# First unit's stacks read in two goes, and the order of the first and last loads, in a four-layer transformer kernel

## The chip, the cores and the metric

The kernel runs on one core of a Trainium2 chip. A core has TensorE (PE in the profile, its weight loads PEld), VectorE (DVE), ScalarE (ACT), GpSimd (POOL) and SyncE (SP), which here only issues transfers; 16 DMA engines move the data. The metric is the device time of one execution of the whole program in microseconds, the median of several runs.

## The reference

Four blocks of attention and feed-forward over x of shape [4, 512, 256] in float32, each with a residual and a layer norm ahead of it. The attentions of L0, L1 and L3 have 16 heads of 16. L0 attends causally to x itself and also to a context of [4, 512, 128], L1 and L3 to the context alone. L2 has two attentions with heads of 32.

```python
x = x + _L0_xattn_ref(_layernorm(x), ctx_512, ...)   # causal self attention + cross attention, 16 heads of 16
x = x + _L0_ffn_ref(_layernorm(x), ...)              # ternary weights, gelu
x = x + _L1_xattn_ref(_layernorm(x), ctx_512, ctx_512, ...)
x = x + _L1_ffn_ref(_layernorm(x), ...)
x = x + _L2_xattn_ref(_layernorm(x), ctx_512, ...)   # two attentions, heads of 32
x = x + _L2_ffn_ref(_layernorm(x), ...)              # gated, then two gelu layers, then out
x = x + _L3_xattn_ref(_layernorm(x), ctx_512, ...)
x = x + _L3_ffn_ref(_layernorm(x), ...)              # fp4 weights and activations
```

## The kernel before

The kernel is written as a plan. `build_program` appends steps (named tuples) to one list in the order in which they are thought of, and each engine's program walks through that list and issues those steps that concern it, each with the semaphores that it waits for. So the order of the list is the order on every engine's queue, SP's included. X holds x as 16 tiles of 128 tokens, four per batch; XT holds the normalised and turned x, ctxT the turned context, and `xn` is a buffer of two halves of four tiles that serves the normalised rows, the context on its way in (the context fills both halves) and much else. `xn_free` says when it may be written again. There are eight PSUM banks: bank_t (six, taken in pairs by the attention), bank_o and bank_m.

At the start, line 254 loads all four batches of x, `load_context` (line 878) loads the context into `xn` and turns it, the weights of L1's attention and the biases of L0's feed-forward are loaded as their buffers are placed, and then `L0_xattn` (line 911) loads its own weights, bias columns and rows. `LazyNorm` (line 334) takes the statistics of batch 0 when it is made (L2076 to L2099 on DVE), normalises it (L2106) into `xn`, adds the output bias to X (L2440 on POOL), and turns it (L1906) into XT. `hold` (a step for the compute engines) makes them wait for a list of loads before anything further.

`attention` (line 420) works through units; with heads of 16 a unit is 8 heads of one batch. For each unit `project_stack` (line 510) projects K or Q into bank_m (L1895), splits it into a high and a low half (L2341 and L2342 on ACT, L2470 on POOL), and writes both to DRAM (`SpillStack`, L2579 and L2580 on SP). `read_stack` (line 538) brings them back as a stack of 48 rows a head, twice (a half for each 64 partitions), in six DMAs for K and six for Q (`ReadStack`, L2589). A stack has four slots; a slot holds the heads of one score step. The scores of a unit for the row maxima (`Smax`, L1956 on PE, L2148 on DVE) go slot by slot and within a slot over four query tiles, through three tiles of two banks. Then the maxima go through DRAM into the stack (L2592, L2599), and the logits (L1970), probabilities (L2355) and values (L2001) follow.

`attention` starts with the two projections of unit 0 and `run_all`, which is where its stacks are spilled and read, and goes on with the maxima of unit 0; between them the chores run, one a tick: the statistics of the other batches (`norm.rest`), the V projections, the stacks of units 1 and 2.

L2's feed-forward (line 1438) works through two pairs of batches; each weight block is loaded by SP two blocks ahead, split by ACT and DVE (L2391, L2232; L2230 scales a block of the output layer), and multiplied. Between the pairs, pair 1 is turned out of `xn`. At its end all engines wait for everything, and L3's attention (line 1579) loads its weights and the context, turns it, and takes the statistics of batch 0.

## Time and profile before

| | |
|---|---|
| median of 3 runs | 3652.71 us (3636.51 to 3660.86) |
| the profiled execution | 3634.89 us, span 3633.1 us |
| PE busy | 2869.3 us, 79% |
| DVE busy | 2040.3 us, 56% |
| ACT busy | 1460.1 us, 40% |
| POOL busy | 1146.9 us, 32% |
| HBM read, written | 130.73 MB, 64.75 MB |
| mean granted clock of PE | 0.864 of full speed |

Busy shares are means over stages that differ. The rows further down are of the timeline (start, duration, engine, line, operation, what it writes and reads, how often; in square brackets how long the engine was idle before it and what released it), of the DMA part of the profile (busy share in 40 slices), of one line's or tile's own page, and of stretches (busy time of each engine, the granted clock, the DMA share).

### The profile page before, as it was taken

The page shows a single profiled execution, that of the slowest core. Times are in us where ns is not written, and L with a number is a line of the kernel's source. Part 1 is how long each engine was busy: PE and PEld are TensorE (multiplying, and loading weights), DVE is VectorE, ACT ScalarE, POOL GpSimd, SP SyncE. Part 2 cuts the span into 40 slices and gives each one's busy share as a digit, 9 for nine tenths or more (in the row PEclk, how much of TensorE's full clock was granted, in tenths as well). Part 3 has the DMA queues.
Part 4 walks back from the last instruction along what each step waited for, and adds up shares of the span by engine and source line. Part 5 has one row for each costly group of instructions (what it writes and reads, how often), then busy time and mean ns, then how long its engine had stood idle before and what let it go on. Part 6 is the DMA issues. An engine that isn't in the chain of part 4 may idle for free. (4 is left out here: it accounts for less than half of the span.)

```text
span 3633.1 us, 44859 instructions
## 1 busy us (share of the span) xinstructions
PE 2869.3 (79%) x16756; PEld 1615.4 (44%) x16756; DVE 2040.3 (56%) x3607; ACT 1460.1 (40%) x1932; POOL 1146.9 (32%) x1007
## 2 busy tenths in 40 slices
PE   4888888658866979999866888877999997588544
PEld 2333333443324534444662344356778776233122
DVE  3445546756634735444784666685454443566587
ACT  1254555415551225444422545432433432266422
POOL 2122322221222225555413768650010110122333
PEclk7599989777886989999987899888999998699666
DMA  5355545024521001111100000000221221564100
GB/s 125 72 114 102 117 101 116 19 48 109 106 70 39 1 18 36 40 40 60 59 7 12 1 1 1 13 12 15 74 76 34 66 61 58 91 117 97 32 10 14
DMA packets 129176, 198.50 MB, mean 55 GB/s; under 512 B 35712, under 2 KB 65921, under 8 KB 128833
## 3 DMA queue, kind: packets, MB, share of 16 engines
q1 hardware_dynamic: 97216, 143.23, 17.4%
q0 software_dynamic: 31744, 52.41, 5.2%
q8 instruction: 134, 2.20, 0.3%
q14 instruction: 82, 0.66, 0.1%
HBM read 130.73 MB, written 64.75 MB: 54 GB/s over the span
## 5 line engine op out<-in xcount | busy, mean ns | idle before, releaser
L2148 DVE TENSOR_REDUCE L_mx<-bank_t 128x2 f32<-128x1024 f32 (+3 forms) x512 | 562.7, 1121 | 492.8 <-PE bank_t L1956 307.8
L2355 ACT ACTIVATE L_P<-bank_t 128x1024 f32<-128x1024 f32 (+2 forms) x512 | 477.9, 945 | 469.9 <-PE bank_t L1970 285.5
L2148 DVE TENSOR_REDUCE L2a_mx<-bank_t 128x2 f32<-128x1024 f32 x256 | 311.4, 1222 | 398.5 <-PE bank_t L1933 397.7
L2355 ACT ACTIVATE L2a_P<-bank_t 128x1024 f32<-128x1024 f32 x256 | 261.6, 1023 | 289.0 <-PE bank_t L1945 288.7
L1956 PE MATMUL bank_t<-L_KS,L_QS 48*128 48x512 f32 (+2 forms) x1024 | 261.7, 514 | 105.6 <-DMA L_QS<-L_spill_q_halves 84.8
L1970 PE MATMUL bank_t<-L_QS,L_KS 50*128 50x512 f32 (+2 forms) x1024 | 241.5, 476 | 108.2 <-DVE L_mx L2148 81.2
L1933 PE MATMUL bank_t<-L2a_QK 32*128 32x512 f32 x1536 | 255.9, 448 | 71.6 <-DVE L2a_mx L2148 35.5
L2001 PE MATMUL bank_o<-L_P,L_V 128*32 128x512 f32 (+3 forms) x2048 | 286.4, 636 | 2.6 <-ACT xn L2362 1.8
L1956 PEld LDWEIGHTS bank_t<-L_KS,L_QS 48*128 48x128 f32 x1024 | 107.5, 209 | 349.9 <-issue 246.5
L1941 PE MATMUL bank_t<-L2a_QK 32*128 32x512 f32 x1536 | 259.4, 447 | 0.0
L1933 PEld LDWEIGHTS bank_t<-L2a_QK 32*128 32x128 f32 x1536 | 138.0, 197 | 236.6 <-issue 105.5
L2470 POOL TENSOR_TENSOR L_lo<-L_full,L_hi 128x512 fp32r<-128x512 f32 x64 | 81.2, 1269 | 449.3 <-ACT L_hi L2342 429.7
L1895 PE MATMUL bank_t<-L2g_act_high,L2g_w_high 128*128 128x512 f32 x472 | 186.8, 396 | 18.8 <-DVE L2g_w_low L2232 16.6
L1970 PEld LDWEIGHTS bank_t<-L_QS,L_KS 50*128 50x128 f32 x1024 | 106.4, 207 | 204.5 <-DVE L_mx L2148 140.4
L2239 DVE TENSOR_TENSOR L2g_act_low<-ctxT,L2g_act_high 128x512 fp32r<-128x512 f32 x96 | 67.4, 703 | 218.2 <-ACT L2g_act_high L2396 218.2
L1895 PE MATMUL bank_t<-L2g_act_high,L2g_w_low 128*128 128x512 f32 x472 | 185.2, 392 | 0.0
L1895 PE MATMUL bank_t<-L2g_act_low,L2g_w_high 128*128 128x512 f32 x472 | 185.2, 392 | 0.0
L2480 POOL TENSOR_TENSOR L2a_sums<-L2a_sums,L2a_P 128x1024 f32<-128x1024 f32 x64 | 153.6, 2400 | 31.2 <-ACT L2a_P L2355 27.1
L2001 PE MATMUL bank_o<-L2a_P,L2a_V 128*32 128x512 f32 (+3 forms) x896 | 141.3, 566 | 1.7 <-ACT L2a_P L2355 1.7
L2475 POOL TENSOR_TENSOR L2a_diag<-L2a_P,after_q 128x256 f32<-128x256 f32 x128 | 94.9, 742 | 143.7 <-issue 80.8
L2005 PE MATMUL bank_o<-L2a_P,ones 128*32 128x512 f32 x512 | 138.0, 616 | 0.0
L1941 PEld LDWEIGHTS bank_t<-L2a_QK 32*128 32x128 f32 x1536 | 130.6, 195 | 13.8 <-issue 10.7
(424 smaller groups left out, 6057.6 us busy)
## 6 DMA issues: line engine op xcount, KB each, us to landing
L_KS<-L_spill_k_halves SPq DMA_DIRECT2D x192, 128.0 KB, 4.6
L_QS<-L_spill_q_halves SPq DMA_DIRECT2D x192, 128.0 KB, 5.2
L_spill_raw<-xn POOLq DMA_DIRECT2D x64, 256.0 KB, 2.5
L2g_raw<-in_L_ffn_h_blocks SPq DMA_DIRECT2D x32, 512.0 KB, 3.8
L_spill_k_halves<-L_hi SPq DMA_DIRECT2D x32, 256.0 KB, 2.0
L_spill_k_halves<-L_lo SPq DMA_DIRECT2D x32, 256.0 KB, 2.3
L_spill_q_halves<-L_hi SPq DMA_DIRECT2D x32, 256.0 KB, 2.5
L_spill_q_halves<-L_lo SPq DMA_DIRECT2D x32, 256.0 KB, 3.1
```

The source lines that it names most:

```text
L1895: mm = e.matmul(out_, w, x, start=first and i == 0, stop=last and i == len(terms) - 1)
L1933: mm = e.matmul(m.tile[:, c, :], Q[r, m.qt * P:(m.qt + 1) * P], K[r, :], start=i == 0, stop=i == 2)
L1941: e.matmul(l.tile[:, c, :], K[r, l.kt * P:(l.kt + 1) * P], Q[r, :], start=i == 0, stop=False)
L1956: mm = e.matmul(m.tile[:, c, 0:n_keys], st.QS[m.un.buf][rows, slot, m.qt * P:(m.qt + 1) * P], st.KS[m.un.buf][rows, slot, 0:n_keys], start ...
L1970: mm = e.matmul(x.tile[:, c, q0:S], st.KS[x.un.buf][rows, slot, x.kt * P:(x.kt + 1) * P], st.QS[x.un.buf][rows, slot, q0:S], start=True, s ...
L2001: mm = e.matmul(bank_o[row:row + 32, q0:q1], V[:, s.kt, head, :], moving, start=s.first and i == 0, stop=s.last and i == len(cuts) - 1, ti ...
L2005: mm = e.matmul(bank_o[row + 32:row + 64, :], ones[:, 0:32], s.at.Pr[pb][:, c, :], start=s.first, stop=s.last, tile_position=(0, row + 32))
L2148: e.tensor_reduce(neg, s.tile[:, :, 0:n_keys], AX.X, ALU.max, negate=True).then_inc(sem(s.done), 1)
L2355: e.activation(s.at.Pr[s.pb][:, :, q0:S], s.tile[:, :, q0:S], ACT.Exp, scale=s.at.scale).then_inc(sem(s.exp), 1)
L2470: e.tensor_tensor(s.low[:, :], s.full, s.high[:, :].bitcast(F32), ALU.subtract).then_inc(sem(s.lo), 1)
L2475: e.tensor_tensor(s.dst[:, :, :], s.src, after_q[:, :].unsqueeze(1).to_broadcast([P, 2, P]), ALU.mult).then_inc(sem(s.done), 1)
L2480: e.tensor_tensor(s.dst[:, :, :], s.a[:, :, :], s.b[:, :, :], ALU.add).then_inc(sem(s.done), 1)
```

## The change

On SP the order of loads becomes: batch 0 of x; L0's Wk, its bias column, Wq, its bias column and the output bias row; batches 1 to 3 of x; L0's other weights, columns and rows; L1's weights (`w.fetch`); L0's feed-forward biases (`follows.fetch`); and the context last (`fetch_context`). Batch 0 is normalised and turned ahead of all but the first six. The compute engines hold for those first loads only; the hold for the rest, and the turning of the context, through bank_m, stand behind unit 0's stack reads (`begun`). In L2's feed-forward the context for L3 is loaded between the two pairs, and the statistics of batch 0 for L3 are taken ahead of the output layer of the second pair. In all attentions with heads of 16, unit 0's stacks are read in two goes: slot 0 of K and of Q first, then slots 1 to 3; the maxima of slot 0 wait for the first go, the others for both.

```diff
-ReadStack = namedtuple("ReadStack", "at un which spill after landing")
+ReadStack = namedtuple("ReadStack", "at un which slots spill after landing")
...
+        self.first_slots, self.stacked_later = None, []
...
-        x_in = [load(X[:, TB * b:TB * b + TB, :], dram["x"][b].rearrange("(t p) c -> p t c", p=P)) for b in range(B)]
+        x_in = []
+
+        def fetch_x(b):
+            x_in.append(load(X[:, TB * b:TB * b + TB, :], dram["x"][b].rearrange("(t p) c -> p t c", p=P)))
+        fetch_x(0)
...
                 if un.n >= st.n and un.n - st.n not in finished:
                     later(1, lambda: read_stack(un, which, written))
                     return
+                after = [written, stack_done.get(un.n - st.n), st.ready[un.buf]]
+                if un.n == 0:
+                    un.first_slots = 1
+                    later(1, lambda: read_slots(un, which, slice(un.first_slots, st.slots), after, un.stacked_later))
+                    read_slots(un, which, slice(0, un.first_slots), after, un.stacked)
+                else:
+                    read_slots(un, which, slice(0, st.slots), after, un.stacked)
+
+            def read_slots(un, which, slots, after, stacked):
                 at_ = landing(n=3 * st.q_of)
-                add(ReadStack(at, un, which, split_dram[which][un.n % 3],
-                              [written, stack_done.get(un.n - st.n), st.ready[un.buf]], at_))
+                add(ReadStack(at, un, which, slots, split_dram[which][un.n % 3], after, at_))
                 spill_read[which, un.n] = at_.done
-                un.stacked.append(at_.done)
+                stacked.append(at_.done)
...
-                step = Smax(at, un, s, qt, tile, [*tiles.free[i_t], *un.stacked], mm,
+                step = Smax(at, un, s, qt, tile, [*tiles.free[i_t], *un.stacked, *([] if s == 0 else un.stacked_later)], mm,
...
             chores += prep(units[0])
             run_all()
+            if begun is not None:
+                begun(misc)
...
+        def fetch_context():
+            return load(ctx_tok, dram["ctx_512"].rearrange("b (t p) c -> p (b t) c", p=P), xn_free)
+
+        def load_context(e_in, ring=None):
             for b in range(B):
-                e_t, e_c = turn([ctx_tok[:, TB * b + i, :] for i in range(TB)], [e_in], "scalar", ctxT[:, b, :])
+                e_t, e_c = turn([ctx_tok[:, TB * b + i, :] for i in range(TB)], [e_in], "scalar", ctxT[:, b, :], ring=ring)
...
-        ctx_ready = load_context()
+        ahead = {}
...
+        def L0_first(scope):
+
+            f = Stage()
+            f.W = {n: sb(scope, f"L0_{n}", [P, KC, C]) for n in ("Wq", "Wk")}
+            f.bq, f.bp = sb(scope, "L0_bcols", [P, 4, KC]), sb(scope, "L0_bp", [P, C])
+            f.loads = [weight_load(f.W["Wk"][:, :, :], "L0_xattn_Wk", KC), load(f.bq[:, 1, :], dram["L0_xattn_bk_cols"]),
+                       weight_load(f.W["Wq"][:, :, :], "L0_xattn_Wq", KC), load(f.bq[:, 0, :], dram["L0_xattn_bq_cols"])]
+            f.e_bp = row_load(f.bp, "L0_xattn_bp")
+            return f
...
+            norm = LazyNorm((first.bp, [first.e_bp]), lambda t: x_in[t // TB])
+            for step in norm.steps(0, ALL):
+                step()
+            xt = norm.ready
+            hold(first.loads)
+            bq, ctx_ready = first.bq, []
+
+            for b in range(1, B):
+                fetch_x(b)
             loads = [weight_load(W[n][:, :, :], f"L0_xattn_{n}", KC) for n in W]
             loads += [weight_load(Wc[n][:, :, :], f"L0_xattn_{n}", 1) for n in Wc]
             loads += [weight_load(Wo[:, :, :], "L0_xattn_Wp", KC)]
...
+            w.fetch()
+            follows.fetch()
+            e_ctx = fetch_context()
+
+            def rest(ring):
+                ctx_ready.append(load_context(e_ctx, ring))
+                hold(loads)
...
                 if pair == 0:
                     e_x = turned_pair(e_normal, e_mm)
+                    ahead["context"] = fetch_context()
+                else:
+                    ahead["norm"] = LazyNorm(None)
                 e_out = output(pair, act[0], [e_h])
...
-            e_ctx = load_context()
-            norm = LazyNorm(None)
+            e_ctx = load_context(ahead["context"])
+            norm = ahead["norm"]
...
-                            e.dma_start(stack[row:row + D, :, :].bitcast(F32), halves[q]).then_inc(sem(s.landing.done), 16)
+                            e.dma_start(stack[row:row + D, s.slots, :].bitcast(F32),
+                                        halves[q][:, s.slots, :]).then_inc(sem(s.landing.done), 16)
```

## Rows read from the trace of the kernel before

**Rows 1.** The page: busy us, share of the span, instructions

```profile
PE 2869.3 (79%) x16756; PEld 1615.4 (44%) x16756; DVE 2040.3 (56%) x3607; ACT 1460.1 (40%) x1932; POOL 1146.9 (32%) x1007
```

**Rows 2.** L0's entry: DMA share in 1.5 us slices of 0:60; timeline

```profile
DMA  0399999999799998100000816999999990000000
...
36.66 2.80 SPq L2589 DMA_DIRECT2D L_KS<-L_spill_k_halves  x6
...
51.27 0.48 PE L1956 MATMUL bank_t<-L_KS,L_QS 48*128 48x128 f32 x2 [18.37 <-DMA L_QS<-L_spill_q_halves]
```

**Rows 3.** Timeline of L1's entry

```profile
769.07 2.76 SPq L2589 DMA_DIRECT2D L_KS<-L_spill_k_halves  x6
...
782.31 1.65 PE L1956 MATMUL bank_t<-L_KS,L_QS 48*128 48x512 f32 x6 [17.20 <-DMA L_QS<-L_spill_q_halves]
...
787.15 0.79 PE L1956 MATMUL bank_t<-L_KS,L_QS 48*128 48x512 f32 x2
...
792.41 0.79 PE L1956 MATMUL bank_t<-L_KS,L_QS 48*128 48x512 f32 x2 [4.46 <-DVE L_mx L2148]
```

**Rows 4.** Timeline of L3's entry

```profile
3066.83 1.76 DVE L2133 MEMSET L_KS<- 32x2048 f32 x1 [0.47 <-issue]
3066.97 0.44 SPq L2576 DMA_DIRECT2D L_Wv<-in_L_xattn_Wv_T  x1
...
3080.54 1.38 DVE L2106 TENSOR_SCALAR xn<-X,mv,rstd 128x256 f32<-128x256 f32 x4 [7.72 <-PE bank_t L1906]
...
3083.74 1.68 PE L1895 MATMUL bank_m<-ctxT,L_Wk 128*128 128x512 f32 x2
...
3086.86 1.98 PE L1895 MATMUL bank_m<-XT,L_Wq 128*128 128x512 f32 x4 [1.44 <-ACT L_hi L2342]
...
3092.60 2.78 SPq L2589 DMA_DIRECT2D L_KS<-L_spill_k_halves  x6
...
3107.61 1.65 PE L1956 MATMUL bank_t<-L_KS,L_QS 48*128 48x512 f32 x6 [18.77 <-DMA L_QS<-L_spill_q_halves]
```

**Rows 5.** Timeline of the program's first 30 us

```profile
4.02 5.10 SPq L2576 DMA_DIRECT2D L_Wq<-in_L_xattn_Wq  x1
5.33 1.40 DVE L2076 BATCH_NORM_STATS2 stats<-X 128x6 f32<-128x256 f32 x4
...
12.95 3.67 PE L1906 MATMUL bank_t<-ident,xn 128*128 128x128 f32 x16 [12.95 <-DMA xn<-in_ctx]
...
16.73 1.38 DVE L2106 TENSOR_SCALAR xn<-X,mv,rstd 128x256 f32<-128x256 f32 x4 [7.20 <-PE bank_t L1906]
...
18.17 1.10 PE L1906 MATMUL bank_t<-ident,xn 128*128 128x128 f32 x8 [1.56 <-DVE xn L2106]
...
19.31 0.69 DVE L2111 COPY XT<-bank_t 128x512 f32<-128x512 f32 x1 [1.19 <-PE bank_t L1906]
...
25.65 3.75 PE L1895 MATMUL bank_m<-XT,L_Wk 128*128 128x512 f32 x4 [6.38 <-DMA L_bp<-in_L_xattn_bp]
```

**Rows 6.** Timeline: the first maxima's way back

```profile
101.19 0.60 SPq L2599 DMA_DIRECT2D L_QS<-L_spill_max_rows  x2
...
108.94 0.79 PE L1970 MATMUL bank_t<-L_QS,L_KS 50*128 50x512 f32 x2 [5.25 <-DMA L_QS<-L_spill_max_rows]
```

**Rows 7.** One line's page: landing of L2592 in 100:600, of L2589 in 0:60

```profile
DMA to landing us min/median/max: 1.7/2.0/2.4
...
DMA to landing us min/median/max: 3.5/4.9/6.2
```

**Rows 8.** One tile's page: L_Wv in 3060:3130

```profile
DMA to landing us min/median/max: 6.4/6.4/6.4
```

**Rows 9.** Timeline between the pairs of L2's feed-forward

```profile
2776.97 1.62 SPq L2576 DMA_DIRECT2D L2g_raw<-in_L_ffn_w_blocks  x2
...
2779.02 0.42 DVE L2230 TENSOR_TENSOR L2g_raw<-L2g_raw,ctxT 128x256 f32<-128x256 f32 x1 [0.83 <-DMA L2g_raw<-in_L_ffn_w_blocks]
```

**Rows 10.** Stretches: PE, PEld, DVE, ACT, POOL busy, PEclk, DMA share, GB/s

```profile
3037.00:3040.00 3.00, 3.00 (x17) 3.00 (x16) 0.76 (x2) 0.00 (x0) 0.00 (x0) 0.55 0.14 44
...
3043.00:3046.00 3.00, 3.00 (x27) 3.00 (x27) 0.76 (x2) 0.42 (x1) 0.00 (x0) 1.00 0.20 56
```

54 lines of the change are left out of this document (25 added, 29 removed).

## The prediction

> **What bounds the kernel now.** I read the busy shares first: TensorE is busy for 79% of the span and no other engine for more than 56% [rows 1]. So a change to data movement can pay only in stretches where TensorE waits for data. I then looked for these in the timeline, at the entry of each of the three attentions with heads of 16 (L0 at 0 us, L1 at 760, L3 at 3064). All three have one shape. TensorE projects the stacks of unit 0, their halves go to DRAM and come back, and TensorE stands still until the last read has landed. From the first issue of the stack read to the first score matmul it takes 36.66 to 51.27 = 14.6 us in L0 [rows 2], 769.07 to 782.31 = 13.2 in L1 [rows 3], and 3092.60 to 3107.61 = 15.0 in L3 [rows 4]. Each score matmul row names the q stack's DMA as what it waited for, 18.4, 17.2 and 18.8 us. Two entries have a second wait ahead of that. In L0 the normalise waits until 16.73 for the turned context, although the statistics were done before, and the K projection waits until 25.65 for the last of some 25 loads [rows 5]. In L3 the normalise waits until 3080.54 in the same way [rows 4]. Nothing can cover these waits, since all later work of the stage descends from unit 0. A microsecond won there should arrive at the end.
>
> **L0, the front.** The order on SP becomes batch 0 of x, five loads (two weights, two bias columns, one row), then the rest, then the context. The statistics start at 5.33 [rows 5], behind two memsets of DVE and the landing of x, and neither moves. Their chain of 4 + 4 + 12 small DVE operations ends by 9.6. The normalise then starts at 9.6 rather than 16.73, because nothing has used xn. It takes 1.38, the turns start 0.06 later, and the K projection could start 1.9 us after the turns' start (18.17 to 20.0, as the second copy of XT shows 0.69 us from 19.31): 9.6 + 1.4 + 0.1 + 1.9 = 13.0. Do the five loads land by then? 1,152 KB are in front of them, issued by 3.6 us at 0.48 us each. The first four x loads (2 MB) took from 0.8 to about 9 us with the queue full, so 1.1 MB is there by 7. Yes. The projection starts at 13.0, 12.6 us earlier than 25.65.
>
> Between K projection and the first stack read lie 36.66 - 25.65 = 11.0 us (projection, halves on ACT and POOL, two spills, SP in order) [rows 2, 5]. That gives 24.1. Here the moved loads matter: the spills share SP's queue with 23 issues that now stand behind the first six and ahead of them. 29 issues at 0.48 us end at about 15, and the context's own issue may hold SP some 5.1 us more, as the row of the load behind it shows [rows 5]: 20. The K spill is ready at 13.0 + 6.8 = 19.8, so SP is just free. The data is another matter. The DMA engines are full from 2 to 22.5 us in the slices of the page over the first 60 us [rows 2], the same 6.3 MB stand in the queue in the new order, and a transfer issued behind others waits for them: the two small reads of the max rows, issued at 101.19 behind a stack read, held TensorE until 108.94 [rows 6]. The K spill then lands near 23 to 25 and the Q spill near 26.5, against a first read at 24.1 that needs only K. I take the first read at 24.5; if the backlog reaches through both spills it is 27.
>
> The Trainium skill (DMA: Bandwidth & Descriptors, section on queues, rings and completion order) says that on each DMA engine the descriptors are consumed in ring order. By that rule the trace agrees, with its 7.7 us for two small reads.
>
> **The context's turns** go into the one bank bank_m and into the wait for the stack read. Sixteen turn matmuls took 3.67 us at 12.95 [rows 5], so one group of four takes 0.92, then a copy on ACT of 0.60 and two hand-overs of about 0.25: 2.0 each, 8 in all. The context lands at about 23.5, so they end at 31.5, just ahead of the first score. They cost nothing as long as that cover holds; without the cover they cost 8. POOL's 10 us of memsets for the other units move behind them, still 20 us ahead of the unit that needs them.
>
> **Two goes, all three stages.** Unit 0 now reads slot 0 of both stacks (12 DMAs of 32 KB) and then slots 1 to 3 (12 of 96 KB). SP's six K reads took 2.80 us [rows 2], 0.467 each, so the twelfth starts 5.1 us after the first. Its data is small: 384 KB at the 1.5 MB in 12 us of the old reads is 3 us, hidden behind the issues. What comes on top is one landing. Between the nearest rows, 32 KB writes of the max rows at 1.7 to 2.4 us and the old 128 KB reads at 3.5 at least [rows 7], I take 2.5. First score after 7.6 us, bounds 6.8 and 8.7. Gains: 14.6 - 7.6 = 7.0 in L0, 5.6 in L1, 7.4 in L3, in all 20.0, bounds 17 to 22. If small transfers do not land sooner than the whole, it is 0.
>
> The second go adds a wait on TensorE ahead of slot 1. It is issued by 11.2 us and lands at about 15, perhaps 1 to 2 us later than the whole did in L1. Slot 1 is wanted 787.15 - 782.31 = 4.8 us after the first score, at 12.4. So TensorE, with one V projection and all later scores queued behind it, stands up to 2.6 us longer there. But the next score tile waits for DVE until 792.41, 10.1 us after the first score [rows 3], which is 17.7 on the new clock: DVE is in the norm statistics of the other batches (8 tiles in L1, 12 in L0 and L3) and needs none of this. The wait is hidden, 0 us, and would cost 2.6 a stage without that DVE work.
>
> A rule of the Trainium skill speaks against the split. DMA: Bandwidth & Descriptors, section Bandwidth, asks for transfers of 1 MiB and calls those under 64 KB dominated by descriptors. By it the first go would gain little; that is the first rival.
>
> **L3, the front.** The context has landed in L2's feed-forward, and the statistics are done there. After the stage's hold, 16 context turns take 3.7 us (3064.2 to 3068) beside the two memsets on DVE, the second of which starts at 3066.83 and takes 1.76 [rows 4]. Normalise 3068.6 to 3070.0, turns and copies 1.9: ready at 3072. Now the weights are late next: L_Wv is issued at 3066.97 and lands 0.44 + 6.4 us later, at 3073.8 [rows 4, 8]. They are ahead of the context in the queue today, so their landing does not change. K projection at 3073.9 in place of 3083.74 (its first weight load is 0.2 earlier): 9.6 us. TensorE has been idle for 2 us by then and ran 24 turns less recently; if the Q projection takes 3.75 us, as K's did in L0 after a pause, and not 1.98 [rows 4, 5], that loses 1.8. I take half, 0.9. L3's front: 8.7.
>
> **What is paid in L2's feed-forward.** The context load stands on SP ahead of a block load. That load went out at 2776.97 and DVE waited 0.83 us for its landing at 2779.02 [rows 9], so there is no slack on DVE and about 0.8 on ACT. SP may be held for 5.1 us after 2773.9, and 1 MB at 300 GB/s is in front: the block comes 2 to 3 us late. TensorE loses 0 to 2.5, I take 1.2, once. The statistics of batch 0 (1.41 + 0.38 + 12 of 0.2 = 4.2 us on DVE) now lie between the last act_low (to 3036.1) and the split of the second output block, which was ready at 3037.4 and wanted at 3040.7. It is ready at 3041.9: 1.2 us, once. Both pauses are short of the one at 3034 to 3036 of 2.2 us, after which the granted clock was 0.55 for 3 us and 1.00 again at 3043 [rows 10].
>
> **Sum.** L0: 25.65 - 13.0 = 12.6, less 0.4 for the spill's landing, plus 7.0 = 19.2. L1: 5.6. L3: 8.7 + 7.4 = 16.1. Paid: 2.4. Net 38.5. The profiled execution took 3634.89 and would take 3596.4; the median of the three runs is 3652.71, 18 us above it, and the median is what will be compared: 3652.7 - 38.5 = 3614. That is 1.05%. About 1% (36.5 us, 3616.2) is what a measurement of this kernel can tell from no change, so the forecast lies on that edge.
>
> **The rivals.**
> *The small go lands with the whole.* The old reads move 1.5 MB in 12 us (131 GB/s), the loads 6.3 MB in 20.5 us (307 GB/s) [rows 2], so something in the reads is slow other than bytes. If it is a cost for each DMA rather than for each packet, 24 DMAs are no faster than 12. Against it: the first of the old reads landed in 3.5 us and the last in 6.2 [rows 7], so DMAs land in turn. The 20.0 are gone: 3634. The skill's rule above comes out here.
> *The backlog in L0.* The queue's order puts both spills and the first read behind the context. First read at 27 to 28, context turns later too, L0 gains 15 instead of 19, or 12 if SP is held at each step: 3618 to 3621.
> *The block loads.* In L2's feed-forward several block loads, not one, come late behind the context, 5.1 us and then 2 more: 3619 to 3622.
> *The other side: the clock.* L2's feed-forward is dense matmul work from 2800 to 3060. If the new pause at 2781 or 3041 made the granted clock fall and stay at its lower level (1.2 GHz), each microsecond of work would cost nearly one more; it takes 45 us at that level to eat the 38, and half of the stretch would give 3730. The row against it is the recovery within 6 us [rows 10].
> *More than forecast.* The waits shrink from 18 to 11 us and context turns keep TensorE busy in L0's, so it returns to its upper level sooner: up to 10 us more, 3604.
>
> **Chances.** All steps as summed 0.50 (3603 to 3624, from the landing's bounds, 3 us a stage, and the median's own scatter). Small go useless 0.12. Backlog 0.17. Block loads 0.10. Clock down 0.03. More than forecast 0.08. Faster by over 1%: half of the first case and a bit more (0.29), all of the last (0.08), and a third of the backlog and block cases, since the three runs spread 24 us (0.09), with some from the scatter of the rest (0.03): 0.49. Slower by over 1%: 0.03. Within: 0.48. Range 3598 to 3636: up to the useless small go, down to the full gain on a median 8 us lower.
>
> **What would show it.** First K projection at 13 us in L0 and at 3073.9 in L3. First score at about 32, 7.6 us after the first stack read, in L0, and the same distance in L1 and L3. No score of slot 1 waiting for a DMA beyond the end of DVE's statistics. The DVE wait at 2779 grown to 3 us. The forecast is wrong if the first score still comes 13 us after the first read, if the K spill lands after 26, or if TensorE's granted clock between 2800 and 3060 is below 0.95.

## The result, and the profile after

The changed kernel took 3623.26 us (median of 9 runs, 3594.24 to 3628.10), the kernel before 3643.07 us beside it (median of 9, 3623.28 to 3660.86). The ratio is 0.994 with a 95% interval of 0.9913 to 0.9967: faster, by 0.3 to 0.9%. Timed again on another occasion it took 3610.65 us against 3656.37 us, ratio 0.9878 (0.9853 to 0.9903). The two intervals do not overlap, so a single ratio of this kernel can be off by more than its own interval says. Keep that in mind for every ratio below; the distances inside the stages repeat far better. The ratios leave out one execution that ran in a slower state (3921.29 us, of the kernel split_pad further down).

The profiled execution took 3623.26 us, its span is 3621.5 us and its mean granted clock 0.865 (before: 3634.89, 3633.1 and 0.864).

The page of the changed kernel, busy times (answers to [rows 1]):

```profile
PE 2887.8 (80%) x16756; PEld 1623.9 (45%) x16756; DVE 2038.2 (56%) x3607; ACT 1459.9 (40%) x1932; POOL 1147.8 (32%) x1007
```

The picture is the same: TensorE is the busiest engine, and no instruction of it was added or removed. L0's entry, from the timeline (columns: start, duration, engine, line, operation, written tile <- read tiles, count, and in brackets the idle time before and what ended it). The first line is the busy share of the DMA engines in 40 slices of the first 60 us:

```profile
DMA  0299699999995599656324799970000000000000
```

```profile
9.56 1.38 DVE L2152 TENSOR_SCALAR xn<-X,mv,rstd 128x256 f32<-128x256 f32 x4
10.99 1.97 PE L1952 MATMUL bank_t<-ident,xn 128*128 128x128 f32 x8 [10.99 <-DVE xn L2152]
13.83 3.75 PE L1941 MATMUL bank_m<-XT,L_Wk 128*128 128x512 f32 x4 [0.87 <-DVE XT L2157]
16.45 0.84 SPq L2622 DMA_DIRECT2D xn<-in_ctx  x1
20.65 0.72 SPq L2625 DMA_DIRECT2D L_spill_k_halves<-L_hi  x1
24.80 0.66 PE L1952 MATMUL bank_m<-ident,xn 128*128 128x128 f32 x4 [2.31 <-DMA xn<-in_ctx]
26.24 2.71 SPq L2635 DMA_DIRECT2D L_KS<-L_spill_k_halves  x6
30.89 0.60 ACT L2370 ACTIVATE ctxT<-bank_m 128x512 f32<-128x512 f32 x1 [1.20 <-PE bank_m L1952]
33.24 0.47 PE L2002 MATMUL bank_t<-L_KS,L_QS 48*128 48x128 f32 x2 [2.39 <-DMA L_QS<-L_spill_q_halves]
```

The K projection starts at 13.83, where it started at 25.65 [rows 5], and its releaser is now the second copy of XT, not a load. The context's turns sit between 24.80 and 31.5, ahead of the first score at 33.24 (51.27 before [rows 2]), and nothing on the path waits for them.

L1's entry, which got the two goes and nothing else (answers to [rows 3]), and what follows it up to the first logits (line L2016):

```profile
740.02 2.76 SPq L2635 DMA_DIRECT2D L_KS<-L_spill_k_halves  x6
747.07 1.65 PE L2002 MATMUL bank_t<-L_KS,L_QS 48*128 48x512 f32 x6 [10.81 <-DMA L_QS<-L_spill_q_halves]
755.78 0.80 PE L2002 MATMUL bank_t<-L_KS,L_QS 48*128 48x512 f32 x2 [3.79 <-DMA L_QS<-L_spill_q_halves]
757.17 0.80 PE L2002 MATMUL bank_t<-L_KS,L_QS 48*128 48x512 f32 x2 [0.59 <-DVE L_mx L2194]
785.01 0.43 SPq L2639 DMA_DIRECT2D L_spill_max_rows<-L_mT  x1
793.04 1.65 PE L2002 MATMUL bank_t<-L_KS,L_QS 48*128 48x512 f32 x6 [9.33 <-DMA L_QS<-L_spill_q_halves]
796.74 0.58 SPq L2646 DMA_DIRECT2D L_QS<-L_spill_max_rows  x2
805.92 0.80 PE L2016 MATMUL bank_t<-L_QS,L_KS 50*128 50x512 f32 x2 [6.58 <-DMA L_QS<-L_spill_max_rows]
```

Three things are to be seen. The first score comes 7.05 us after the first read instead of 13.2 (12.2 in another execution of the kernel before). The predicted wait ahead of slot 1 is there (3.79 us, at 755.78), and it costs nothing: the next tile starts at 757.17, 10.10 us after the first score, exactly the distance of before (782.31 to 792.41 [rows 3]). But the last two waits are longer than before: 9.33 us for unit 1's stack and 6.58 us for the max rows, from the max rows' read to the first logits 9.18 us. In the trace of the kernel before the same places were:

```profile
825.24 1.65 PE L1956 MATMUL bank_t<-L_KS,L_QS 48*128 48x512 f32 x6 [6.50 <-DMA L_QS<-L_spill_q_halves]
...
828.91 0.58 SPq L2599 DMA_DIRECT2D L_QS<-L_spill_max_rows  x2
...
832.56 0.79 PE L1970 MATMUL bank_t<-L_QS,L_KS 50*128 50x512 f32 x2 [1.02 <-DMA L_QS<-L_spill_max_rows]
```

L3's entry (answers to [rows 4]):

```profile
3069.93 2.05 PE L1941 MATMUL bank_m<-ctxT,L_Wk 128*128 128x512 f32 x2 [0.98 <-DVE XT L2157]
3073.41 3.69 PE L1941 MATMUL bank_m<-XT,L_Wq 128*128 128x512 f32 x4 [1.44 <-ACT L_hi L2388]
3080.87 2.70 SPq L2635 DMA_DIRECT2D L_KS<-L_spill_k_halves  x6
3087.84 1.65 PE L2002 MATMUL bank_t<-L_KS,L_QS 48*128 48x512 f32 x6 [10.74 <-DMA L_QS<-L_spill_q_halves]
```

First score 3087.84 against 3107.61, with the kernel 3.2 us ahead when the stage began. Two tables collect what the rows say in every profile of this study. The three distances are L0: start of the program to the first P (first ACT row of the probabilities); L1: K projection to first P; L3: from the last time that ACT splits activations in L2's feed-forward (`L2g_act_high`, 3034.78 before and 3030.58 now) to the first P. All in us.

| kernel (label) | L0 | L1 | L3 | sum |
|---|---|---|---|---|
| before | 110.1 | 72.8 | 121.5 | 304.4 |
| before, another execution (before_again) | 111.4 | 72.7 | 121.5 | 305.6 |
| changed | 91.6 | 75.0 | 103.9 | 270.5 |
| changed, another execution (after_again) | 88.7 | 73.9 | 104.5 | 267.2 |

The two executions of one kernel agree within 1.3 us in L1 and L3 and within 2.9 in L0, although the spans of the two executions of before are 38 us apart. The change wins 20.6 us in L0 and 17.3 in L3, and loses 1.7 in L1 (means of the two).

Part of the scatter has a place, and goes with the granted clock. From the first score to the spill of the max rows, L0 took 38.3 to 39.0 us in the executions whose mean granted clock in that stretch was 0.76 or 0.77, and 40.4 to 41.5 us where it was 0.66 or 0.67 (the changed kernel's 0.66, its other execution 0.77; only two_units, further down, lies outside, with 42.0 us at 0.74). L3 took 31.9 to 32.5 us at 0.61 to 0.66, and 33.8 to 34.5 us at 0.55. The stretch in L3, before and in the changed kernel (busy us and counts of PE, PEld, DVE, ACT, POOL, then the granted clock, the DMA share and GB/s):

```profile
3107.60:3141.50 33.90, 21.31 (x58) 9.76 (x58) 27.64 (x59) 4.89 (x8) 2.53 (x2) 0.55 0.29 57
```

```profile
3087.80:3119.80 32.00, 18.92 (x58) 9.10 (x58) 27.53 (x59) 4.91 (x8) 3.95 (x3) 0.61 0.52 97
```

TensorE does the same 58 matmuls in 18.9 us instead of 21.3. In L3 2.0 of the 17.3 us are this. The shorter length also comes in split_only and fronts_only and the longer one in four kernels that have the whole change, so it is not shown to belong to the change.

### The profile page after: what moved, and what is told of

Same layout as the page of the kernel before. It is cut to its first block and busy times, and to the rows that moved or that the text cites. A ratio compares the mean times of both kernels' runs of the same rounds, so it can differ in the third digit from the quotient of the medians.

```text
span 3621.5 us, 44902 instructions
## 1 busy us (share of the span) xinstructions
PE 2887.8 (80%) x16756; PEld 1623.9 (45%) x16756; DVE 2038.2 (56%) x3607; ACT 1459.9 (40%) x1932; POOL 1147.8 (32%) x1007
## 3 DMA queue, kind: packets, MB, share of 16 engines
q1 hardware_dynamic: 97792, 143.23, 17.3%
## 5 line engine op out<-in xcount | busy, mean ns | idle before, releaser
L2016 PE MATMUL bank_t<-L_QS,L_KS 50*128 50x512 f32 (+2 forms) x1024 | 240.4, 473 | 117.7 <-DVE L_mx L2194 88.1
L1979 PEld LDWEIGHTS bank_t<-L2a_QK 32*128 32x128 f32 x1536 | 137.8, 198 | 234.5 <-ACT L2a_P L2401 103.9
L2016 PEld LDWEIGHTS bank_t<-L_QS,L_KS 50*128 50x128 f32 x1024 | 106.3, 206 | 213.2 <-DVE L_mx L2194 147.8
```

Of the source, the lines that this page charges most:

```text
L1979: mm = e.matmul(m.tile[:, c, :], Q[r, m.qt * P:(m.qt + 1) * P], K[r, :], start=i == 0, stop=i == 2)
L2016: mm = e.matmul(x.tile[:, c, q0:S], st.KS[x.un.buf][rows, slot, x.kt * P:(x.kt + 1) * P], st.QS[x.un.buf][rows, slot, q0:S], start=True, s ...
```

## The experiments

**First set: does each entry keep what it wins, and is the sum of the parts the whole?** The first theory (A) was that it does, and that what is missing in the timing is scatter of the granted clock in the long attentions. The rival (B) was that part is given back at the next transfers. Four kernels: the changed one again, the two goes alone, the fronts alone, and the kernel before again.

The changed kernel once more (after_again):

> The changed kernel once more, for a second profile and more times beside the same chip's runs of before. Theory A (each entry keeps what it won, and what is missing of the 38 us is scatter of the clock): about 0.9895 to 0.992 of before. Theory B (part of the gain is given back at the next transfers, the way of the first maxima and unit 1's stacks): 0.993 to 0.995, and from L1's first score to its first probabilities it again takes 55 us or more, where before took 51. Both expect the first score 7.1 us after the first stack read in all three stages.

Measured: 3610.65 us, ratio 0.9878 (0.9853 to 0.9903). L1 from first score to first P: 58.6 us. The ratio fits neither (A had 0.9895 at the least); the 58.6 us fit B.

The two goes alone (split_only):

```diff
+                after = [written, stack_done.get(un.n - st.n), st.ready[un.buf]]
+                if un.n == 0:
+                    un.first_slots = 1
+                    later(1, lambda: read_slots(un, which, slice(un.first_slots, st.slots), after, un.stacked_later))
+                    read_slots(un, which, slice(0, un.first_slots), after, un.stacked)
+                else:
+                    read_slots(un, which, slice(0, st.slots), after, un.stacked)
```

> Before with one part of the change: unit 0's stacks in two goes, all loads in the old order. Both theories expect the first score 7 to 7.5 us after the first stack read where before took 13 to 15. Theory A: 20 us less, 0.9945. Theory B: 8 to 14 us less, 0.996 to 0.998, since what is given back lies behind the first score and hangs on the reads' order.

Measured: 3623.02 us, ratio 0.9904 (0.9888 to 0.9919), by that 35 us under the kernel before, more than either theory had. L0 101.2, L1 67.5, L3 114.0: the entries win 9.5, 5.3 and 7.5 us, 22 in all. L1 takes 52.2 us from first score to first P, as before (51.1 and 52.0). So the two goes are not what B says they are: alone, they give nothing back in L1.

The fronts alone (fronts_only):

```diff
-                if un.n == 0:
+                if False:
```

> The change with unit 0's stacks read in one go (so 12 transfers of 128 KB as before): only the order of the loads, the early statistics and the early context. Theory A: L0 12 us and L3 9 us earlier at the first score, less 2 to 3 us in L2's feed-forward: 18 us less, 0.995. Theory B expects the same here, since a mere shift changes no order of the reads behind the first score. If the fronts alone give under 10 us, the loss lies in them.

Measured: 3639.20 us, ratio 0.9963 (0.9938 to 0.9988), 13.5 us. L0 98.4, L1 80.1, L3 114.4. L0 and L3 win 12.4 and 7.1 us. L1, in which this kernel changes not one instruction, loses 7.3: 58.5 us from first score to first P. Neither theory had that. The loss in L1 goes with the fronts, not with the two goes.

The kernel before once more (before_again):

> The kernel before once more, for a second profile: what one stage takes from its first score to its first probabilities, and how far the stages differ between two executions of one kernel. Theory A: L1's 51 and L3's 49 us come again within 5 us either way, and stages differ by clock alone. Theory B: they come again within 1 us.

Measured: 3673.27 us in its profiled execution, span 3671.5 against 3633.1. The entries are within 1.3 us of the first execution; the long stretch of L0's attention behind them is not. The windows view (busy us of PE, PEld, DVE, ACT, POOL with counts, granted clock, DMA share, GB/s) from L0's first P to about its last, of the one execution and of the other:

```profile
110.00:655.00 545.00, 483.45 (x2767) 197.52 (x2770) 286.24 (x375) 274.60 (x363) 138.98 (x173) 0.85 0.46 100
```

```profile
111.00:666.00 555.00, 493.77 (x2766) 200.64 (x2764) 286.32 (x375) 274.77 (x362) 139.14 (x172) 0.84 0.45 98
```

In a stretch that is 10 us longer, TensorE is 10.3 us longer busy with the same matmuls (2,767 and 2,766), at a slightly lower granted clock. L3's attention differs by 10.5 us too (first P to last P 254.9 against 244.4). That is the noise under every timing here, and theory A's half that held.

**Second set: why L1 pays, and whether the max rows can be had sooner.** One thing that the fronts change in L1 is where its tiles lie. The tiles of L0's first weights (`L0_first`: two weights of 2,048 bytes of each partition, a bias tile and a row) are allocated ahead of L1's weights and live until L1 ends, so that L1's tiles, and the stacks of L0, lie 5,152 bytes higher in SBUF. The other things are the order and the time of the loads. Two kernels tell these apart.

L0's first weights given back when L0's attention ends (first_closed), so that L1's tiles lie as before the change:

```diff
         with ExitStack() as outer:
-            first, w = L0_first(outer), L1_weights(outer)
+            w = L1_weights(outer)
             norm, side = LazyNorm((w.bo, w.loads), lambda t: out_ready[t], False), Side()
-            attention_and_ffn(lambda scope, keep, follows: L0_xattn(scope, keep, follows, first, w),
-                              lambda keep: L0_ffn(keep, side, norm))
+            with ExitStack() as inner:
+                first = L0_first(inner)
+                attention_and_ffn(lambda scope, keep, follows: L0_xattn(scope, keep, follows, first, w),
+                                  lambda keep: L0_ffn(keep, side, norm))
```

> The changed kernel, but the tiles of L0's first weights (two 512x512 weights, two small ones: 18.5 KB of every partition) are allocated behind L1's weights and given back when L0's attention ends, so that L1's tiles lie where they lay before the change; no instruction is changed. Open is why L1, in the two kernels that have the early loads of L0, takes 58 to 60 us from its first score to its first P, where the kernels without them take 51 to 52 (max rows read to first P 8.4 to 10 us against 4.5 to 5.5). Theory place: the transfers into the stacks are slower because the tiles lie 18.5 KB higher. Then here L1 takes 51 to 53.5 us from first score to first P, a 2 KB packet takes under 0.15 us in the 15 us before the first P, and the time is 5 to 8 us under the changed kernel's. Theory order: it is the order or the time of the transfers. Then it stays at 58 to 60 us and the time stays the changed kernel's within 3 us.

(The size in that text and in the next one, and the 512x512, are wrong: it is 5,152 bytes. x has 256 columns.) Measured: 3606.50 us, ratio 0.9881 (0.9846 to 0.9916). L1 took 55.9 us from first score to first P, 71.2 from its K projection: between what the two theories expected.

The other direction (split_pad): the kernel with the two goes alone and an unused tile of the same 5,152 bytes.

```diff
         with ExitStack() as outer:
+            pad = sb(outer, "pad", [P, 2 * KC * C + 4 * KC + C])
             w = L1_weights(outer)
```

> The kernel before with the two goes alone, and with one unused tile of 18.5 KB a partition allocated ahead of L1's weights; no instruction is changed beside the split. Theory place (tiles that lie 18.5 KB higher make L1's transfers slow): L1 takes 58 to 60 us from first score to first P, where the same kernel without the unused tile took 52.2, and the time is 5 to 8 us over its 0.9904, so 0.992 to 0.9925. Theory order: 51 to 53.5 us, and the time is that of the kernel without the tile, 0.9904 within 0.002.

Measured: 3636.16 us, ratio 0.9946 (0.9915 to 0.9976). L1 takes 59.6 us from first score to first P, 74.9 from its K projection, where the same kernel without the unused tile took 52.2 and 67.5. No instruction differs, only addresses. Place holds in this direction with its full size of 7.4 us. One reservation: the two were profiled once each and on different chips. L1 was slow with the higher tiles on three chips; with the lower ones and the loads in their old order it was fast in all three profiles, none of which is known to be from split_pad's chip. The timeline of L1 without the tile and with it:

```profile
803.73 0.49 SPq L2601 DMA_DIRECT2D L_spill_max_rows<-L_mT  x1
808.76 1.65 PE L1965 MATMUL bank_t<-L_KS,L_QS 48*128 48x512 f32 x6 [6.58 <-DMA L_QS<-L_spill_q_halves]
812.53 0.58 SPq L2608 DMA_DIRECT2D L_QS<-L_spill_max_rows  x2
817.17 0.79 PE L1979 MATMUL bank_t<-L_QS,L_KS 50*128 50x512 f32 x2 [2.11 <-DMA L_QS<-L_spill_max_rows]
```

```profile
795.74 0.43 SPq L2602 DMA_DIRECT2D L_spill_max_rows<-L_mT  x1
804.04 1.65 PE L1966 MATMUL bank_t<-L_KS,L_QS 48*128 48x512 f32 x6 [9.44 <-DMA L_QS<-L_spill_q_halves]
807.80 0.58 SPq L2609 DMA_DIRECT2D L_QS<-L_spill_max_rows  x2
816.68 0.79 PE L1980 MATMUL bank_t<-L_QS,L_KS 50*128 50x512 f32 x2 [6.35 <-DMA L_QS<-L_spill_max_rows]
```

The two longer waits of the changed kernel are here, 9.44 and 6.35 us, without its loads. The windows view of the last 15 us ahead of L1's first P (the last two numbers are the DMA engines' busy share and the GB/s that they moved), first the kernels whose L1 tiles lie low: before, split_only, first_closed.

```profile
818.00:833.00 15.00, 5.88 (x20) 2.63 (x20) 7.00 (x8) 1.87 (x2) 0.00 (x0) 0.52 0.92 238
```

```profile
803.00:818.00 15.00, 5.66 (x18) 2.84 (x20) 8.01 (x7) 1.11 (x2) 0.00 (x0) 0.50 0.87 220
```

```profile
797.00:812.00 15.00, 5.93 (x20) 2.93 (x20) 8.01 (x7) 0.27 (x1) 0.00 (x0) 0.50 0.90 163
```

Then those that lie 5 KB higher: the changed kernel and split_pad.

```profile
792.00:807.00 15.00, 5.90 (x20) 2.94 (x20) 8.01 (x7) 0.24 (x1) 0.00 (x0) 0.50 0.87 132
```

```profile
802.00:817.00 15.00, 5.14 (x16) 2.39 (x18) 8.02 (x7) 0.00 (x0) 0.00 (x0) 0.50 0.91 145
```

The DMA engines are equally busy, 0.87 to 0.92, but move 132 to 145 GB/s instead of 220 to 238: the same packets take longer. Worked out from the trace's DMA packets in those 15 us, one of 2,048 bytes takes 0.122 and 0.126 us in the first two, 0.176 in first_closed, 0.207 and 0.199 in the last two. So the mean packet follows the wait. That first_closed lands between says that place is not all of it in these 15 us; what else slows its packets there was not found. L0's stacks were moved by the same 5,152 bytes, and there the mean packet in the last 15 us did not change (0.167 us in split_only, 0.164 in split_pad).

Unit 2's stacks behind unit 0's max rows (unit2_later). In L1's rows of the changed kernel the max rows were spilled at 785.01 and read back only at 796.74, where the reads of unit 2's stacks, which are needed much later, stood ahead on SP's queue:

```diff
-                if un.n >= st.n and un.n - st.n not in finished:
+                if (un.n >= st.n and un.n - st.n not in finished) or (un.n == 2 and 0 not in max_in):
                     later(1, lambda: read_stack(un, which, written))
```

> The changed kernel, with the reads of unit 2's stacks put behind the read of unit 0's max rows on SyncE's queue, in L0, L1 and L3. Theory queue (the max rows wait in the DMA queues behind unit 2's stacks, which nobody wants yet): from the max rows' read to the first P 3 to 4.5 us in all three stages, where it was 6.1, 10.0 and 7.6, so the first P comes 2 to 3, 5 to 7 and 3 to 4 us earlier after the first score, and the time is 10 to 14 us under the changed kernel's. Rival, given back: unit 2's first score then waits for its stacks, TensorE stands 5 us or more there, and the time is the changed kernel's within 3 us; the wait of unit 2's scores would show it.

Measured: 3597.74 us, ratio 0.9847 (0.9811 to 0.9883). From first score to first P: L0 53.5, L1 53.2, L3 48.7 us (changed kernel: 58.3, 59.7, 46.6; its other execution 55.4, 58.6, 46.5). L1, from the timeline:

```profile
793.07 0.43 SPq L2639 DMA_DIRECT2D L_spill_max_rows<-L_mT  x1
800.94 1.65 PE L2002 MATMUL bank_t<-L_KS,L_QS 48*128 48x512 f32 x6 [9.14 <-DMA L_QS<-L_spill_q_halves]
801.91 0.55 SPq L2646 DMA_DIRECT2D L_QS<-L_spill_max_rows  x2
802.55 2.66 SPq L2635 DMA_DIRECT2D L_KS<-L_spill_k_halves  x6
807.58 0.80 PE L2016 MATMUL bank_t<-L_QS,L_KS 50*128 50x512 f32 x2 [0.34 <-DVE L_mx L2194]
```

The max rows go back 8.8 us after their spill instead of 11.7, and the first logits wait for DVE, no longer for a DMA. The theory had the distance too short, though: from the max rows' read to the first P it expected 3 to 4.5 us and got 6.1, 6.5 and 7.8, where the changed kernel has 6.1, 10.0 and 7.6. Counted from the max rows' spill to the first P, the edit won 2.4 us in L0, all of it ahead of the read, and 6.4 in L1, 2.9 ahead of the read and 3.5 behind it. In L3 it won nothing (14.66 us against 14.64). The rival, that unit 2 would then wait for its stacks, did not come: in the 100 us around and behind L1's first P TensorE waited 0.7 us for a stack in the changed kernel and not at all here.

Both together (closed_later):

> The two together: L1's tiles where they lay before the change, and unit 2's stacks read behind unit 0's max rows. If place and queue both hold, L1 takes 50 to 52 us from its first score to its first P, with 3 to 4.5 us from the max rows' read, and the time is 12 to 20 us under the changed kernel's. If only queue holds, the time is that of the kernel with the later reads alone, within 3 us; if neither, the changed kernel's.

Measured: 3594.10 us, ratio 0.9845 (0.9812 to 0.9877). Its L1 takes 49.7 us from first score to first P, the shortest of the study, and its entries sum to 260.8 us against 271.6 in first_closed, the same kernel without the later reads. Its median is 12.4 us below that one's, timed side by side; the two intervals overlap, so the timing alone does not separate them.

**Third set: is it alignment?** 5,152 is no multiple of 64; 5,184 is. The first stack of L1 begins at byte 89,600 of each partition in the kernel before, a multiple of 64, and at 94,752 in the changed kernel, 32 bytes off one. L3's begins at 109,280 in all kernels so far, also 32 bytes off. Three kernels with unused tiles:

```diff
-            pad = sb(outer, "pad", [P, 2 * KC * C + 4 * KC + C])
+            pad = sb(outer, "pad", [P, 2 * KC * C + 4 * KC + C + 8])
```

> The kernel before with the two goes alone and an unused tile of 5,184 bytes of each partition ahead of L1's weights. The unused tile of the earlier kernel had 5,152 bytes (the texts that went with the earlier kernels called it 18.5 KB, which was worked out wrongly: x has 256 columns, so that two weights are 4 KB): it put L1's stacks on addresses that are no multiple of 64, and L1 took 59.6 us from first score to first P instead of 52.2. This one puts them 32 bytes higher, on multiples of 64. Theory alignment: 51 to 54 us, mean time of a 2 KB packet in the 15 us before L1's first P under 0.14 us. Rival height (5 KB higher is what counts): 58 to 60 us and 0.19 to 0.21 us. The time: alignment 0.990 to 0.992, height 0.9946 within 0.003.

Measured: 3630.12 us, ratio 0.9961 (0.9937 to 0.9984). L1 59.1 us, and the window of its last 15 us moves no more than before:

```profile
808.00:823.00 15.00, 5.13 (x16) 2.37 (x18) 8.01 (x7) 0.00 (x0) 0.00 (x0) 0.50 0.93 150
```

Alignment to 64 bytes falls for L1. The rival expected what came, 59 us; but it isn't the only reading left, as the end of this set shows.

```diff
+            pad = sb(outer, "pad", [P, 8])
             first, w = L0_first(outer), L1_weights(outer)
...
+        pad = sb(ctx, "pad3", [P, 8])
         Gt, Ut = sb(ctx, "L3f_GT", [P, KC, FF], BF16), sb(ctx, "L3f_UT", [P, KC, FF], BF16)
```

> The changed kernel with two unused tiles of 32 bytes a partition, one ahead of L0's first weights, one ahead of L3's tiles, so that the stacks of L0, L1 and L3 begin on multiples of 64 bytes (L3's did not in any kernel so far). Theory alignment: L1 takes 52 to 56 us from first score to first P where the changed kernel took 59.7 and 58.6, L3 42 to 44 us where it took 46.6, with packets under 0.15 us in the 15 us before its first P (0.172 so far), and the time is 8 to 12 us under the changed kernel's. Rival height: nothing of L1 or L3 moves by over 1.5 us, and the time is the changed kernel's.

Measured: 3605.84 us, ratio 0.9885 (0.9867 to 0.9902). L1 59.2 us: the changed kernel's. In L3 the packets did get faster (0.141 us in the 15 us before the first P; 0.169 to 0.175 where L3 was not moved, and 0.163 in two_units), and it gained nothing: from the max rows' spill to the first P it took 14.65 us, the changed kernel 14.64. (The 49.1 us from first score to first P, against 46.6, are L3's longer length ahead of that spill, at a granted clock of 0.55.) So a move of 32 bytes changed how long packets take in L3 and not in L1, and alignment to 64 is not the rule that sorts them.

The same with the later reads (later_aligned):

> The kernel whose unit 2 stacks are read behind unit 0's max rows, with the two unused tiles of 32 bytes. It took 53.5, 53.2 and 48.7 us from first score to first P in L0, L1 and L3, and 0.9847 of the kernel before. Theory alignment: L1 49 to 51 us, L3 44 to 46 us, and the time 0.981 to 0.983. Rival height: L1 53 within 1.5 us, L3 48.7 within 1 us, and the time 0.9847 within 0.003.

Measured: 3598.90 us, ratio 0.9864 (0.9843 to 0.9885), 6.9 us below the aligned kernel beside it. L0 53.5, L1 52.8, L3 46.6 us. L1 is again that of the higher tiles. From first score to first P this is 1.8, 6.4 and 2.5 us less than in the aligned kernel; but L3's 2.5 lie ahead of the max rows' spill, at another granted clock (0.61 against 0.55). From the spill to the first P the later reads won 2.2, 6.3 and 0.0 us.

No kernel was built for a coarser alignment, but the kernels at hand differ in it. The first stacks of L1 begin on a multiple of 256 bytes when they lie low (89,600), and not when they lie high (94,752 or 94,784). L3's do so only in the two kernels of this set that moved them by 32 bytes (109,312, where all others have 109,280), and L0's in none. Worked out from the trace's DMA packets, the mean time of a 2,048-byte packet between 60 and 230 us behind the stage's first stack read (5,200 to 6,600 packets each) is:

| first stack begins | L0 | L1 | L3 |
|---|---|---|---|
| on a multiple of 256 bytes | - | 0.153 to 0.162 us (6 profiles) | 0.163 and 0.165 us (2) |
| elsewhere | 0.166 to 0.173 us (14) | 0.173 to 0.182 us (8) | 0.176 to 0.186 us (12) |

This sorts all profiles of L1 and of L3, first_closed too (0.153), and it has a reason for L0, whose stacks lay off such a multiple before and after. Height can't explain L3, where 32 bytes did it. A multiple of 128 doesn't do: L0's stacks begin on one in three kernels, at 0.166, 0.166 and 0.167 us. So 256 bytes is the reading that fits best; that it is the cause is not shown, since no run moved L1's tiles from one multiple of 256 to another.

**Last: unit 1 in two goes as well** (two_units), on top of closed_later:

```diff
-                if un.n == 0:
+                if un.n <= 1:
```

> The kernel with both edits (L1's tiles where they lay before the change, unit 2's stacks behind unit 0's max rows) and unit 1's stacks read in two goes as well, slot 0 ahead of the others. Unit 1's first score waits for its stack in all three stages (in L1 5.8 us, until 5.2 us behind the last issue of the read). Theory transfer (that wait is for bytes that the first score does not need): it falls by 2 to 4 us in each stage, and the time is 6 to 12 us under that of the kernel without the third edit (0.9845), so 0.981 to 0.983. Rival, issue: twelve more issues of 0.46 us stand on SyncE's queue ahead of the spill and the read of unit 0's max rows, 5.5 us, and the first P, which waits for the max rows, comes 2 to 5 us later after the first score in each stage (54.9, 49.7 and 48.6 us without the edit); the time is the same within 3 us or up to 12 us more.

Measured: 3594.10 us, ratio 0.9884 (0.9853 to 0.9915) beside a kernel before of 3635.03. The median is that of closed_later to the hundredth, and the ratio is 0.4% worse, with intervals that overlap. From first score to first P: 53.6, 51.1 and 46.5 us (54.9, 49.7, 48.6 without the edit), 2.0 us less in sum, which is no more than the step of L3's clock (0.66 against 0.55 from first score to spill). TensorE's waits for the stacks' DMA in L1's entry (total us, how many, the longest), first without the edit, then with it:

```profile
PE bank_t L2004 <- DMA L_QS<-L_spill_q_halves: 20.0, 3, 10.8
```

```profile
PE bank_t L2004 <- DMA L_QS<-L_spill_q_halves: 22.8, 4, 10.8
```

One wait more and the sum larger. Neither theory's size came: no 6 us gained, none lost. The rows show two shifts against each other: in L1 the max rows' spill goes out 2.6 us later behind the first score (the issues), and the read follows it after 3.9 us instead of 5.3.

The table of the entries, for all kernels of these sets:

| label | L0 | L1 | L3 | sum | ratio |
|---|---|---|---|---|---|
| split_only | 101.2 | 67.5 | 114.0 | 282.7 | 0.9904 |
| split_pad | 102.6 | 74.9 | 113.8 | 291.3 | 0.9946 |
| split_pad_64 | 100.7 | 74.4 | 113.8 | 288.8 | 0.9961 |
| fronts_only | 98.4 | 80.1 | 114.4 | 292.8 | 0.9963 |
| aligned | 89.2 | 74.4 | 106.9 | 270.5 | 0.9885 |
| first_closed | 92.9 | 71.2 | 107.6 | 271.6 | 0.9881 |
| unit2_later | 87.2 | 68.5 | 106.9 | 262.6 | 0.9847 |
| later_aligned | 87.2 | 68.1 | 104.0 | 259.3 | 0.9864 |
| closed_later | 88.4 | 65.0 | 107.4 | 260.8 | 0.9845 |
| two_units | 87.2 | 66.4 | 104.3 | 257.9 | 0.9884 |

Against the mean of the two executions of before, 305.0, these sums forecast gains of 22, 14, 16, 12, 34, 33, 42, 46, 44 and 47 us. The ratios times 3,650 give 35, 20, 14, 14, 42, 43, 56, 50, 57 and 42. The order agrees roughly, two_units apart. Single kernels are up to 14 us off, in both directions, but in eight of the ten the ratio says more than the entries, and over all ten by 6 us on average; what lies behind the entries and gives that was not found.

## Why the prediction was right, and where not

The forecast was 3614 us (3598 to 3636) from a median of 3652.7, a ratio of 0.9894. Measured were 3623.26 with 0.994, and 3610.65 with 0.9878. The time fell in the range and the direction held. The size in the first timing falls in "within 1%", in the second in "faster by over 1%": the edge on which the text had put it. That the total came out near is in part luck: one stage lost 7.3 us against its sum, and the others came out above theirs by 3.8 in total, 2.0 of it by L3's clock.

**L0, the front.** Forecast K projection at 13.0, measured 13.83. The statistics ended and the normalise started at 9.56 as worked out (9.6), and no load was late. The term that was small is the turns: eight took 1.97 us at 10.99, as TensorE's first work, and not the 1.10 of [rows 5]. The first read was forecast at 24.5 and came at 26.24, 12.4 us after the K projection instead of 11.5 as summed. What held it was the Q projection, whose spill stands ahead of it on SP's queue: it took 3.38 us, where it was 1.98 in the kernel before (3.78, and 12.8 us in all, in the other execution of the kernel before).

The backlog was there all the same. The K spill went out at 20.65, 6.8 us behind the projection as summed, but its second half landed 4.6 us after its issue, at 26.03, where the text had 23 to 25 and called "after 26" a sign that the forecast is wrong. In the kernel before that half landed after 2.35 us (35.19). The page of the line of the second halves, K's and Q's, in 0:40 of the changed kernel:

```profile
DMA to landing us min/median/max: 2.4/3.5/4.6
```

In the changed kernel this cost nothing, as the Q projection hid it. In the three kernels with the fronts in which that projection took 1.98 us, the first read waited for the K spill, until 27.64, 26.91 and 26.53 (fronts_only, first_closed, closed_later). So the rival's mechanism was real, and the read could hardly have come much before 26. The slices of [rows 2] would have said so: the DMA engines are busy until 24 us there, and the text read 22.5. The context was there at 24.8 (forecast 23.5), and its turns took 6.7 us (forecast 8), so that their end at 31.5, to the tenth, is two misses that cancel. The first score came 18.0 us earlier than before; 19.2 were summed.

**Two goes.** First score 7.0, 7.05 and 7.0 us after the first read in L0, L1 and L3, in every kernel with the edit within 0.3 us (forecast 7.6, bounds 6.8 to 8.7). The landing behind the twelfth issue was the term on the large side: about 1.9 us and not 2.5. The wait ahead of slot 1 came (3.79 us in L1) and was covered by DVE, as argued. The rival of the useless small go is refuted by these rows. The rule on transfer size in the Trainium skill (DMA: Bandwidth & Descriptors, section Bandwidth) did not decide here: 384 KB in 7.0 us are dearer by the byte than 1.5 MB in 13.2, and yet the score came 6 to 8 us sooner, since the wait was for the last landing and not for bytes.

**L1.** This is the step that failed. The sum had 5.6 us for L1 and nothing against it. The entry won 6.2 us (13.2 to 7.05) and lost 8.6 behind it, 51.1 to 59.7 us from first score to first P (in the other executions 12.2 to 7.1, and 52.0 to 58.6). The text let a won microsecond "arrive at the end" once the first score was out, and it had no term for where tiles lie. The unused tile shows the cause as to place: 7.4 us in L1 from tiles that lie 5,152 bytes higher, by slower stack packets, which hold up unit 1's stack and the max rows. Why those addresses are slower stays open. It isn't alignment to 64 bytes (split_pad_64, aligned); a start off a multiple of 256 bytes fits every profile, and was not tested by itself. Moving L1's tiles back won about 3 us of the 7 (first_closed), so that something else in the new order takes part.

**L3, the front.** The K projection was forecast 9.6 us earlier within the stage; measured from TensorE's last matmul of the feed-forward, it comes after 12.1 and 12.7 us instead of 22.75 in both executions before, 10.3 us less. That the weights would be the next wait held in one execution of the two (1.82 us for L_Wv in the other execution; none in the first). The Q projection took 3.69 us where 1.98 were before; the text had charged half of that difference, and all of it came. Read to first score went from 15.0 to 7.0. L3 as a whole won 17.3 us, after the 1.0 that the statistics cost in L2's feed-forward; forecast were 16.1 less 1.2. Up to the first score it won 15.2, near the 14.9, and of the other 2.1 the clock's step is 2.0.

**What was paid in L2's feed-forward.** DVE's wait for the block that stands behind the context load had 0.83 us [rows 9] and was to grow to 3:

```profile
2772.10 0.42 DVE L2276 TENSOR_TENSOR L2g_raw<-L2g_raw,ctxT 128x256 f32<-128x256 f32 x1 [3.28 <-DMA L2g_raw<-in_L_ffn_w_blocks]
```

It grew to 3.28, one block came late and not several, and the context's issue held SP for 0.76 us, not 5.1. In the same place the next split of activations comes 32.1 to 32.6 us behind the one before in all nine profiles with the early context, and 30.5 in the five without: 1.7 us paid, of the 0 to 2.5 with 1.2 taken. For the statistics, TensorE waits ahead of the second output block:

```profile
3037.41 0.38 PE L1941 MATMUL bank_t<-L2g_w_high,L2g_act_high 128*128 128x256 f32 x1 [0.78 <-DVE L2g_w_low L2278]
```

From the last split of activations to TensorE's last matmul the feed-forward takes 27.2 us in those nine profiles and 26.2 in the five: 1.0 us paid, 1.2 forecast. The granted clock (the number before the last two) recovers at once (answers to [rows 10]):

```profile
3034.00:3037.00 3.00, 2.63 (x15) 2.43 (x14) 2.12 (x13) 0.42 (x1) 0.00 (x0) 0.68 0.00 0
3037.00:3040.00 3.00, 2.59 (x21) 2.59 (x22) 1.54 (x4) 0.42 (x1) 0.00 (x0) 1.00 0.23 67
```

Between 2800 and 3050 it is 0.98. So the rival of the clock is out. Together 2.7 us were paid, 2.4 forecast. The rival's other side, that shorter waits would bring TensorE back to its upper level sooner, came in L3 if at all (0.61 and 0.66 against 0.55 up to the max rows' spill, 2 us) and not in L0 (0.66 and 0.77 against 0.77 twice).

**The sum.** L0 20.6 (19.2 forecast), L1 -1.7 (5.6), L3 17.3 (14.9, the statistics paid), together 36.2 us, less 1.7 for the late block: 34.5 where the net was 38.5. The entries are right to 1.4 and 2.4 us in two stages and off by 7.3 in the third. What differs between the timings of one kernel is larger than that and lies in the long attentions. For L0's stretch of 500 us the kernel before and the changed one show

```profile
100.00:600.00 500.00, 443.42 (x2552) 185.16 (x2550) 256.76 (x303) 236.90 (x319) 125.27 (x153) 0.86 0.49 102
```

```profile
100.00:600.00 500.00, 444.37 (x2628) 184.03 (x2624) 267.83 (x332) 250.47 (x335) 131.26 (x162) 0.89 0.49 106
```

at a granted clock of 0.86 and 0.89, with 3% more matmuls done. (The window holds the last 10 us of the entry in the kernel before and none of it in the changed one.) The other executions of the two have 0.83 and 0.90. First P to last P of L0 is 544.8 and 555.1 us in the two executions of before and 533.1 and 534.2 in those of the changed kernel, but also 541.9 and 534.5 in split_only and split_pad, which have the same instructions, and 528.7 to 547.0 in the other kernels with the change. Whether the change itself lifts the clock there is not shown.

## What to carry to other kernels

Where an engine waits for the last of many transfers, put the part that the first instruction needs ahead of the rest: small transfers cost more by the byte, but they land sooner, and the rest is free if another engine's work covers it. Then look at what the next wait is and what stands ahead of it on the queue: here reads that nobody wanted yet stood in front of the max rows, and moving them behind was worth 8 to 10 us, counted from the max rows' spill to the first P in L0 and L1 together. Judge edits of 5 us by the distances inside the stage, which repeat to 1 to 3 us, rather than by the time of a kernel whose long stretches wander by 10, and compare also the stages that you did not edit, since a new tile moves every tile allocated after it.

## What the runs showed that was not expected

- The SBUF addresses of tiles alone changed the speed of the transfers into them: 5,152 or 5,184 bytes higher, the DMA engines moved 145 and 150 GB/s instead of 220 ahead of L1's first P, 0.87 to 0.93 busy in all cases, and that P came 7 us later. A move of 32 bytes shortened the mean packet ahead of L3's first P from about 0.172 to 0.141 us and did nothing in L1. Over 170 us of L1 and of L3, the mean packet took about 0.02 us less in the profiles in which the stacks begin on a multiple of 256 bytes, none of which overlaps with the others; no run tested that by itself.
- One kernel, timed on two occasions beside the kernel before, gave ratios of 0.994 (0.9913 to 0.9967) and 0.9878 (0.9853 to 0.9903).
- In L2's feed-forward the two small payments (1.7 and 1.0 us) can be read off to 0.5 us in every profile, though the stage's length scatters by 7 us: a distance between two rows close around the edit shows what the stage hides.
- The version of the study with the lowest ratio, by a margin within the intervals, reads unit 2's stacks behind unit 0's max rows and gives L0's first weights back before L1: 3594.10 us, 0.9845 (0.9812 to 0.9877) of the kernel before.
